# Probabilities times values in four 64x64 tiles of the array, the heads of a pair swapped for the second sequence

## The chip, the cores and the metric

The kernel runs on one core of one Trainium2 chip. The metric is the device time of one execution in microseconds (us). The engines are named as in the profile: PE is TensorE (PEld its weight loads), ACT is ScalarE, DVE is VectorE, POOL is GpSimd, SP is SyncE, which issues the transfers (SPq: the time it spends on issuing them).

## The reference, cut to what matters

Two attentions (streams a and c), a scan between them (stream b) and a mixture of experts (also stream c) run over 64 sequences of 64 positions with 256 features, all in float32. Each attention has 16 query heads of 64 and one shared key and value head, and one extra "null" key and value per sequence:

```python
sim = jnp.einsum('bhid,bjd->bhij', q, k) * SCALE + attn_bias   # masked
attn = jax.nn.softmax(sim, axis=-1)                            # (b, 16, 64, 65)
out = jnp.einsum('bhij,bjd->bhid', attn, v)                    # the product changed here
out = out.transpose(0, 2, 1, 3).reshape(b, n, INNER)
out = ln(out @ Wout, g_out)
```

## The kernel before

A tile of work is two sequences (`BT` = 2), 128 tokens on the 128 partitions; there are 32 tiles. The work is a software pipeline written out by hand: `ORDER` lists for every engine the steps of one iteration as `stream.step@lag`, and iteration i runs each step on tile i - lag, so five tiles are under way at once. Iterations 0 to 4 and the last four are unrolled, the middle is a loop. `Progress` counts the results of each engine and stream; a step waits until the count says that what it needs is there. `TURNS` gives the order in which steps use each of the eight PSUM banks, and after `>` the result of the engine that empties it; `Banks.free` (L251) turns that into a wait at the start of a PE step.

The steps around the change, in one iteration:

- PE: `... c.ex3 a.xt b.gt b.E0 a.O0 a.O1 b.E1 b.E2 b.E3 b.G a.kv a.W b.m0 b.m1 c.PT0 c.PT1 b.m2 c.O0 c.O1 b.m3 c.eb c.W b.yT`.
- ACT: `... a.PT0 a.PT1 b.BT a.xnT b.E0 a.O0 b.E0u a.O1 b.E1 c.expm b.E2 b.E3 c.prob c.PT0 c.PT1 c.O0 c.O1 a.rstd2`.

For an attention, `PT` (PE, L689) transposes the probabilities of eight pairs of heads, so that the partitions hold (head of the pair, key position); ACT copies them to `X.PT` (L946 to L951). DVE step `V` (L1175) puts the values of each sequence twice on the diagonal of a 128x128 block, in two instructions of 64 partitions. `PV(b)` (PE, L701, the product at L707) multiplies for sequence b that 128x128 block (stationary) with 128x512 of `X.PT` (moving: 8 pairs of heads by 64 positions) into bank `O{b}`; half of the products are with zeros. A float32 matmul is two instructions in the trace. `PV(b)` of ACT (L953 to L959) takes bank `O{b}`, all 128 partitions and 512 columns, to `X.OT`, adding the null value. `W` (PE, L711, L715) waits for ACT's `O1` and multiplies `X.OT` by the output weights in 8 matmuls.

Three turns of the banks matter. Bank 2 goes from `a.O0` to `b.E2`, once ACT's `O0` is done. Bank 1 holds `a.O1`. Bank 6 goes from `c.O0` to `c.eb` (L853), once ACT's `O0` is done. `b.E` (L784) are sums over log decays, `b.m` (L795) the products of the scan, `c.eb` the expert biases.

Of the neighbours: `BT` of ACT copies bank `b.gt` out in one copy of 128 partitions (L1034) and four of 32 (L1037), `b.E0`, `b.E1` ... are exponentials (L1050, `E0u` L1042), `c.prob` (L944) is the softmax exponential of stream c. It leads to DVE's sum and reciprocal (`den`, L1238 to L1243), to POOL's normalisation (`norm`, L1549) and to `c.PT0` (PE, L696). `qr` (ACT, L930 to L935) is the reciprocal norm of the queries of stream c, used by DVE's `c.S0` (L1213). `scores` (PE, L675, L683) already uses matmuls with 64 stationary columns, which write alternately to the partitions 0 to 63 (first sequence) and 64 to 127 (second). The biases are loaded by SP before the pipeline starts (L522, L579) and folded with the null bias by POOL (`fold_bias`, L1593).

Of the kernel before, what the change touches and what calls it, by code (L numbers as in the profile page):

```python
# [28 lines left out]
P = 128  # L29
# [29 lines left out]
def constants():  # L59
# [36 lines left out]
    for name, a in parts.items():  # L96
# [11 lines left out]
        b.bc@2 a.PT0@1 a.PT1@1 c.ex3@4 a.xt@0 b.gt@2 b.E0@2 a.O0@1 a.O1@1 b.E1@2 b.E2@2 b.E3@2  # L108
        b.G@2 a.kv@0 a.W@1 b.m0@2 b.m1@2 c.PT0@3 c.PT1@3 b.m2@2 c.O0@3 c.O1@3 b.m3@2 c.eb@4
# [31 lines left out]
        c.ks@3>dve.ks b.bc@2>dve.Ct a.xt@0>act.xnT a.kv@0>dve.V1 c.PT0@3>act.PT0 c.W@3>dve.cn""",  # L141
    1: """
        b.x@2>dve.xi c.xt@3>act.xnT c.kv@3>dve.V1 b.a@2>act.ae a.PT0@1>act.PT0 a.O1@1>act.O1
        b.yT@2>act.yT""",
    2: """
        b.z@2>dve.zi a.PT1@1>act.PT1 a.O0@1>act.O0 b.E2@2>act.E2 a.W@1>dve.cn""",
# [5 lines left out]
        c.PT1@3>act.PT1 c.O1@3>act.O1""",  # L152
# [4 lines left out]
        b.out@3>dve.x1 c.qs@3>dve.qs c.O0@3>act.O0 c.eb@4>dve.out""",  # L157
# [107 lines left out]
def build(nc, x, out, ins, consts_dram, consts_at):  # L265
    NT = x.shape[0] * x.shape[1] // P
    ctx = ExitStack()
    with ctx:
# [21 lines left out]
        for X, s in ((A, "a"), (C, "c")):  # L290
# [5 lines left out]
            X.null_bias = sb(f"{s}_null_bias", [P, H])  # L296
            X.bias = sb(f"{s}_bias", [P, H, S])
# [11 lines left out]
            X.V = sb(f"{s}_V", [P, BT, P])  # L309
# [136 lines left out]
        def load(eng, s, dst, src):  # L446
# [16 lines left out]
                                             for name in ("x_loaded", "xres_loaded", "out_stored"))  # L463
        A.bias_folded, C.bias_folded = sem("bias_folded_a"), sem("bias_folded_c")
# [35 lines left out]
        def _(sp):  # L500
# [3 lines left out]
            def load_weights():  # L504
# [65 lines left out]
            def position_bias():  # L570
# [7 lines left out]
                for b in range(BT):  # L578
                    sp.dma_start(C.bias[b * S:(b + 1) * S, :, :], skewed).then_inc(mlp_dma, 16)  # L579
# [32 lines left out]
        def _(pe):  # L612
# [9 lines left out]
            def attention(X):  # L622
# [78 lines left out]
                def PV(b):  # L701
                    def run(t):
                        pe.wait_ge(*banks.free(f"{s}.O{b}", t))
                        if b == 0:
                            pe.wait_ge(*dve.at("V1", t))
                            pe.wait_ge(*act.at("PT1", t))
                        pe.matmul(bank(f"O{b}")[:, :], X.V[:, b, :], X.PT[:, :, b * S:(b + 1) * S],  # L707
                                  start=True, stop=True).then_inc(p.done(f"O{b}"), 1)
                    return run

                def W(t):  # L711
                    pe.wait_ge(*banks.free(f"{s}.W", t))
                    pe.wait_ge(*act.at("O1", t))
                    for hp in range(HP):
# [5 lines left out]
                        "S1": scores(1), "PT0": PT(0), "PT1": PT(1), "O0": PV(0), "O1": PV(1), "W": W}  # L720
# [170 lines left out]
        def _(act):  # L891
# [6 lines left out]
            def attention(X):  # L898
# [23 lines left out]
                def q(half):  # L922
                    def run(t):
                        act.wait_ge(*p.at(f"q{half}", t))
                        act.wait_ge(*p.at("O1", t - 1))
                        act.copy(X.qT[:, 4 * half:4 * half + 4, :], banks[f"{s}.q{half}"][:, :])\  # L926
                           .then_inc(a.done(f"q{half}"), 1)
                    return run

                def qr_(t):  # L930
# [4 lines left out]
                    act.activation(qr[:, :], qr_l[:, :], ACT.Exp, scale=-0.5).then_inc(a.done("qr"), 1)  # L935
# [191 lines left out]
        def _(dve):  # L1127
# [7 lines left out]
            def attention(X):  # L1135
# [19 lines left out]
                def K(t):  # L1155
# [19 lines left out]
                def V(t):  # L1175
                    dve.wait_ge(*p.at("kv", t))
                    dve.wait_ge(*p.at("O1", t - 1))
# [24 lines left out]
                def scores(half):  # L1202
                    def run(t):
# [7 lines left out]
                        else:  # L1211
                            dve.wait_ge(*act.at("qr", t))
# [186 lines left out]
            def setup_weights(X, prep, scale):  # L1399
                for k in range(KD):  # L1400
# [20 lines left out]
            def setup_a():  # L1421
# [100 lines left out]
        def _(pool):  # L1522
# [70 lines left out]
            def fold_bias(X):  # L1593
                done = X.bias_folded
                pool.tensor_tensor(X.bias[:, :, :], X.bias[:, :, :],
                                   X.null_bias[:, :].unsqueeze(2).broadcast_to([P, H, S]), ALU.subtract)\
# [13 lines left out]
            def setup_c():  # L1610
                pool.wait_ge(ld_c, n_ld[ld_c.name])
                pool.wait_ge(mlp_dma, 16 + 16 * BT)
# [37 lines left out]
```

## Time and profile before

| | |
|---|---|
| three runs | 1917.19, 1923.50, 1925.61 us (median 1923.50) |
| profiled execution | 1921.49 us, its span 1919.7 us |
| mean granted TensorE clock | 0.966 of 2.4 GHz |
| PE busy | 1751.2 us (91% of the span), 11407 matmul instructions |
| PE weight loads | 1373.9 us (72%) |
| DVE / ACT / POOL busy | 1276.9 (67%) / 807.7 (42%) / 893.5 us (47%) |
| chain that ended last, by engine | PE 86%, DVE 4%, issue 3%, ACT 3%, POOL 2%, SPq 2% |
| L707 on that chain | part of PE's; its matmuls are busy for 61.9 us (a) and 62.2 us (c) |

A row of the timeline gives the start in us from the span's start, the duration, the engine, the line, the operation, out<-in by tile names, the stationary size (rows*columns) and the moving size for a matmul, xN for N instructions merged, and in brackets how long the engine had been idle and what ended that. The durations of pipelined instructions overlap: the next one starts before the one ahead of it ends.

### The profile page before, as it was taken

The page shows a single profiled execution, that of the slowest core. Times are in us where ns is not written, and L with a number is a line of the kernel's source. Part 1 is how long each engine was busy: PE and PEld are TensorE (multiplying, and loading weights), DVE is VectorE, ACT ScalarE, POOL GpSimd, SP SyncE. Part 2 cuts the span into 40 slices and gives each one's busy share as a digit, 9 for nine tenths or more (in the row PEclk, how much of TensorE's full clock was granted, in tenths as well). Part 3 has the DMA queues.
Part 4 walks back from the last instruction along what each step waited for, and adds up shares of the span by engine and source line. Part 5 has one row for each costly group of instructions (what it writes and reads, how often), then busy time and mean ns, then how long its engine had stood idle before and what let it go on. Part 6 is the DMA issues. An engine that isn't in the chain of part 4 may idle for free.

```text
span 1919.7 us, 37680 instructions
## 1 busy us (share of the span) xinstructions
PE 1751.2 (91%) x11407; PEld 1373.9 (72%) x11407; DVE 1276.9 (67%) x2684; ACT 807.7 (42%) x1943; POOL 893.5 (47%) x552
## 2 busy tenths in 40 slices
PE   2378999999999999999999999999999999999875
PEld 1256777777777777777777777778777777787644
DVE  3555766777777667777776667777766677776542
ACT  1134344444444444444444444444444444444321
POOL 1025445555544445555444555554445555544341
PEclk9678999999999999999999999999999999999986
DMA  7110000000000000000000000000000000000000
GB/s 210 53 25 6 2 10 10 9 9 5 4 9 9 9 9 9 9 6 3 9 9 9 9 9 9 6 2 9 9 9 9 9 9 7 1 9 7 6 4 5
DMA packets 40185, 26.52 MB, mean 14 GB/s; under 512 B 19786, under 2 KB 38226, under 8 KB 40148
## 3 DMA queue, kind: packets, MB, share of 16 engines
q1 hardware_dynamic: 40148, 26.05, 5.4%
q8 instruction: 20, 0.33, 0.1%
q14 instruction: 17, 0.14, 0.0%
HBM read 21.33 MB, written 4.71 MB: 14 GB/s over the span
## 4 chain that ended last, share of the span: by engine, by line
PE 86%; DVE 4%; issue 3%; ACT 3%; POOL 2%; SPq 2%; DMA 0%; POOLq 0%; DVEq 0%; ACTq 0%
PE bank L715 12%; PE bank L661 12%; PE bank L618 8%; PE bank L620 7%; PE bank L619 7%; PE bank L683 6%; PE bank L795 6%; PE bank L707 4%; PE bank L696 3%; PE bank L810 3%; PE bank L671 3%; PE bank L784 3%; PE bank L644 2%; PE bank L639 2%; SPq L448 2%
## 5 line engine op out<-in xcount | busy, mean ns | idle before, releaser
L1543 POOL TENSOR_TENSOR a_prob<-a_prob,a_mask 128x1024 f32<-128x1024 f32 x32 | 76.2, 2382 | 264.5 <-DVE a_prob L1209 264.5
L1582 POOL TENSOR_TENSOR y<-y,u 128x512 f32<-128x512 f32 x128 | 162.4, 1269 | 54.1 <-DVE u L1331 49.1
L1331 DVE TENSOR_TENSOR u<-bank,Ef 128x512 f32<-128x512 f32 x128 | 88.5, 691 | 135.8 <-PE bank L795 135.8
L1529 POOL TENSOR_TENSOR c_prob<-c_qT 128x1024 f32<-128x1024 f32 x32 | 82.3, 2573 | 160.4 <-ACT c_qT L926 160.4
L1562 POOL TENSOR_TENSOR resid<-xres,a_c 128x256 f32<-128x256 f32 x32 | 23.6, 738 | 267.8 <-DVE x L1339 215.5
L661 PE MATMUL bank<-a_xnT,a_wq 128*128 128x128 f32 x1024 | 129.2, 281 | 10.2 <-DVE gate_w_lo L1417 10.2
L795 PE MATMUL bank<-u,Gm 128*128 128x512 f32 x256 | 130.9, 613 | 7.8 <-DVE Gm L1323 4.5
L661 PEld LDWEIGHTS bank<-a_xnT,a_wq 128*128 128x128 f32 x1024 | 126.0, 198 | 13.3 <-issue 10.4
L1574 POOL TENSOR_TENSOR u<-xe,Ef 128x512 f32<-128x512 f32 x96 | 122.8, 1294 | 0.0
L715 PE MATMUL bank<-c_wo,c_prob 128*128 128x256 f32 x512 | 121.4, 391 | 0.0
L715 PE MATMUL bank<-a_wo,a_prob 128*128 128x256 f32 x512 | 119.1, 386 | 1.7 <-ACT Ef L1050 1.7
L661 PE MATMUL bank<-c_xnT,c_wq 128*128 128x128 f32 x1024 | 119.6, 275 | 0.0
L661 PEld LDWEIGHTS bank<-c_xnT,c_wq 128*128 128x128 f32 x1024 | 116.9, 192 | 0.0
L618 PE MATMUL bank<-w_e_hi,cT_hi 128*128 128x512 f32 x256 | 114.6, 448 | 0.7 <-ACT c_qT L926 0.7
L715 PEld LDWEIGHTS bank<-c_wo,c_prob 128*128 128x128 f32 x512 | 96.3, 193 | 23.7 <-issue 10.0
L1534 POOL TENSOR_TENSOR c_prob<-c_prob,c_bias 128x1024 f32<-128x1024 f32 x32 | 80.7, 2520 | 58.3 <-DVE c_prob L1213 58.3
L1549 POOL TENSOR_TENSOR a_prob<-a_prob,a_rden 128x1024 f32<-128x1024 f32 x32 | 61.4, 1918 | 98.0 <-DVE a_mask L1227 95.3
L949 ACT COPY c_qT<-bank 128x512 f32<-128x512 f32 x64 | 34.5, 589 | 172.4 <-PE bank L696 172.4
L715 PEld LDWEIGHTS bank<-a_wo,a_prob 128*128 128x128 f32 x512 | 94.6, 190 | 16.2 <-ACT Ef L1050 2.5
L620 PE MATMUL bank<-w_e_hi,cT_lo 128*128 128x512 f32 x256 | 102.2, 399 | 0.0
L619 PE MATMUL bank<-w_e_lo,cT_hi 128*128 128x512 f32 x256 | 101.8, 398 | 0.0
L1309 DVE TENSOR_TENSOR nl_lo<-yT,nl_hi 128x512 fp32r<-128x512 f32 x32 | 86.9, 2717 | 0.0
(289 smaller groups left out, 4658.1 us busy)
## 6 DMA issues: line engine op xcount, KB each, us to landing
a_xin<-in_x SPq DMA_DIRECT2D x32, 128.0 KB, 2.6
xres<-in_x SPq DMA_DIRECT2D x32, 128.0 KB, 2.5
out<-acc SPq DMA_DIRECT2D x32, 128.0 KB, 1.7
a_wq<-in_L_cond_Wq SPq DMA_DIRECT2D x1, 1024.0 KB, 5.0
a_wo<-in_L_cond_Wo SPq DMA_DIRECT2D x1, 1024.0 KB, 7.0
c_wq<-in_L_cond_Wq SPq DMA_DIRECT2D x1, 1024.0 KB
c_wo<-in_L_cond_Wout SPq DMA_DIRECT2D x1, 1024.0 KB
u<-in_L_ffn_expert_w SPq DMA_DIRECT2D x3, 256.0 KB, 3.9
```

Of the source, the lines that this page charges most:

```text
L618: pe.matmul(out, lhs[0][:, k, :], rhs[0], start=first, stop=False)
L619: pe.matmul(out, lhs[0][:, k, :], rhs[1], start=False, stop=False)
L620: return pe.matmul(out, lhs[1][:, k, :], rhs[0], start=False, stop=last)
L661: mm = pe.matmul(bank(f"q{half}")[:, m * P:(m + 1) * P], X.wq[:, k, hp * P:(hp + 1) * P], X.xnT[:, k, :], start=k == 0, stop=k == KD - 1)
L683: mm = pe.matmul(bank(f"S{half}")[b * S:(b + 1) * S, m * P:(m + 1) * P], X.qT[:, 4 * half + m, b * S:(b + 1) * S], X.K[:, b, :], start=Tru ...
L715: mm = pe.matmul(bank("W")[:, 0:D], X.OT[:, hp, :], X.wo[:, hp, :], start=hp == 0, stop=hp == HP - 1)
L795: pe.matmul(banks[f"b.m{l}"][:, :], Gm[:, l, :], u[l][:, :], start=True, stop=True).then_inc(p.done(f"m{l}"), 1)
L1309: dve.tensor_tensor(nl_parts[1][:, :], nl[:, :], nl_parts[0][:, :].bitcast(F32), ALU.subtract)\
L1331: dve.tensor_tensor(tm[l][:, :], banks[f"b.m{l}"][:, :], Ef[l][:, :], ALU.mult)\
L1529: pool.tensor_tensor(qsq[:, :, :], X.qT[:, :, :], X.qT[:, :, :], ALU.mult)\
L1574: pool.tensor_tensor(u[l][:, :], xi[:, :], (E0u if l == 0 else Ef[l])[:, :], ALU.mult)\
L1582: pool.tensor_tensor(y[:, :], y[:, :], tm[l][:, :], ALU.add).then_inc(g.done(f"y{l}"), 1)
```

## The change

The product becomes four matmuls of 64x64 stationary values by 64x512 of probabilities, one for each sequence and head of a pair; the values are stored once. For the second sequence the two heads of each pair change sides from the scores on, so that its products land on the other half of the partitions: key block, bias table, null bias and query norm are laid out for that. PE's two steps `O0` and `O1` become one step `O`, and a matmul of 32x64 by one column stands ahead of the four. ACT empties each bank in two instructions of 64 partitions.

```diff
 ORDER pe
-        ... b.E0@2 a.O0@1 a.O1@1 b.E1@2 ...   ... b.m2@2 c.O0@3 c.O1@3 b.m3@2 c.eb@4
+        ... b.E0@2 a.O@1 b.E1@2 ...           ... b.m2@2 c.O@3 b.m3@2 c.eb@4
 RESULTS act
-            "qr": "qr_l qr",
+            "qr": "qr_l qr0 qr1 qr2", "O0": "O00 O01", "O1": "O10 O11",
 TURNS
-        1: ... a.O1@1>act.O1       2: ... a.O0@1>act.O0      4: ... c.O1@3>act.O1      6: ... c.O0@3>act.O0
+        1: ... a.O1@1>act.O11      2: ... a.O0@1>act.O01     4: ... c.O1@3>act.O11     6: ... c.O0@3>act.O01
...
-            X.V = sb(f"{s}_V", [P, BT, P])
+            X.V = sb(f"{s}_V", [P, BT, DH])
...
-                    load(sp, ld_a, A.bias[part, :, :], ins["fside_16xSxS_0"].rearrange("h i j -> i h j"))
+                    table = ins["fside_16xSxS_0"].rearrange("h i j -> i h j")
+                    for n in range(1 + b):
+                        load(sp, ld_a, A.bias[part, n:H:1 + b, :], table[:, b - n:H:1 + b, :])
...
-                    sp.dma_start(C.bias[b * S:(b + 1) * S, :, :], skewed).then_inc(mlp_dma, 16)
+                    for n in range(1 + b):
+                        sp.dma_start(C.bias[b * S:(b + 1) * S, n:H:1 + b, :], skewed[:, b - n:H:1 + b, :])\
+                          .then_inc(mlp_dma, 16)
...
-                def PV(b):
-                    def run(t):
-                        pe.wait_ge(*banks.free(f"{s}.O{b}", t))
-                        if b == 0:
-                            pe.wait_ge(*dve.at("V1", t))
-                            pe.wait_ge(*act.at("PT1", t))
-                        pe.matmul(bank(f"O{b}")[:, :], X.V[:, b, :], X.PT[:, :, b * S:(b + 1) * S],
-                                  start=True, stop=True).then_inc(p.done(f"O{b}"), 1)
-                    return run
+                def PV(t):
+                    pe.wait_ge(*banks.free(f"{s}.O0", t))
+                    pe.wait_ge(*banks.free(f"{s}.O1", t))
+                    pe.wait_ge(*dve.at("V", t))
+                    pe.wait_ge(*act.at("PT1", t))
+                    pe.matmul(bank("O0")[0:DH, 0:1], X.V[0:32, 0, :], X.PT[0:32, 0, 0:1], start=True, stop=True)
+                    for b in range(BT):
+                        for half in range(2):
+                            rows, side = slice(half * S, (half + 1) * S), half if b == 0 else 1 - half
+                            mm = pe.matmul(bank(f"O{half}")[side * DH:(side + 1) * DH, :], X.V[rows, b, :],
+                                           X.PT[rows, :, b * S:(b + 1) * S], start=True, stop=True)
+                    mm.then_inc(p.done("O"), 1)
...
-                    pe.wait_ge(*act.at("O1", t))
+                    pe.wait_ge(*act.at("O11", t))
...
-                    act.activation(qr[:, :], qr_l[:, :], ACT.Exp, scale=-0.5).then_inc(a.done("qr"), 1)
+                    for n, (part, heads, of) in enumerate(((slice(0, S), slice(0, H), slice(0, H)),
+                                                           (slice(S, P), slice(0, H, 2), slice(1, H, 2)),
+                                                           (slice(S, P), slice(1, H, 2), slice(0, H, 2)))):
+                        act.activation(qr[part, heads], qr_l[part, of], ACT.Exp, scale=-0.5)\
+                           .then_inc(a.done(f"qr{n}"), 1)
...
-                def PV(b):
+                def PV(half):
                     def run(t):
-                        act.wait_ge(*p.at(f"O{b}", t))
-                        act.activation(X.OT[:, :, b * S:(b + 1) * S],
-                                       banks[f"{s}.O{b}"][:, :].rearrange("p (h i) -> p h i", h=HP),
-                                       ACT.Identity, bias=nv_col[:, :]).then_inc(a.done(f"O{b}"), 1)
+                        act.wait_ge(*p.at("O", t))
+                        for b in range(BT):
+                            side = half if b == 0 else 1 - half
+                            part = slice(side * DH, (side + 1) * DH)
+                            act.activation(X.OT[part, :, b * S:(b + 1) * S],
+                                           banks[f"{s}.O{half}"][part, :].rearrange("p (h i) -> p h i", h=HP),
+                                           ACT.Identity, bias=nv_col[part, :]).then_inc(a.done(f"O{half}{b}"), 1)
                     return run
...
-                        dst = X.K[part, :, half * S:(half + 1) * S]
+                        dst = X.K[part, :, :].rearrange("p b (q j) -> p (b q) j", j=S)[:, half:4 - half:3 - 2 * half, :]
...
-                    for half in range(2):
-                        part = slice(half * S, (half + 1) * S)
-                        dve.tensor_tensor(X.V[part, :, half * DH:(half + 1) * DH],
-                                          banks[f"{s}.kv"][part, P:2 * P].rearrange("p (b n) -> p b n", b=BT),
-                                          nv_row[part, :].unsqueeze(1).broadcast_to([S, BT, DH]),
-                                          ALU.subtract).then_inc(d.done(f"V{half}"), 1)
+                    dve.tensor_tensor(X.V[:, :, :], banks[f"{s}.kv"][:, P:2 * P].rearrange("p (b n) -> p b n", b=BT),
+                                      nv_row[:, :].unsqueeze(1).broadcast_to([P, BT, DH]),
+                                      ALU.subtract).then_inc(d.done("V"), 1)
...
             def setup_weights(X, prep, scale):
+                for part, heads, of in ((slice(0, S), slice(0, H), slice(0, H)),
+                                        (slice(S, P), slice(0, H, 2), slice(1, H, 2)),
+                                        (slice(S, P), slice(1, H, 2), slice(0, H, 2))):
+                    mm = dve.tensor_copy(X.null_swapped[part, heads], X.null_bias[part, of])
+                mm.then_inc(X.null_ready, 1)
...
-                dve.memset(A.V[:, :, :], 0.0)
-                dve.memset(C.V[:, :, :], 0.0)
...
             def fold_bias(X):
+                pool.wait_ge(X.null_ready, 1)
```

The rest of the diff renames the results that are waited for (`V1` to `V`, `O1` to `O`, `qr` to `qr2`) and reads `null_swapped` in `fold_bias`.

## Rows read from the trace of the kernel before

**Rows 1.** Windows, one iteration: busy us (instructions) of PE, PEld, DVE, ACT, POOL, clock.

```profile
740.00:794.80 54.80, 53.50 (x358) 42.17 (x357) 38.94 (x82) 24.97 (x60) 27.72 (x18) 1.00 0.02 7
```

**Rows 2.** Timeline of PE in that iteration, around `a.O0` and `a.O1`.

```profile
786.63 0.44 PE L632 MATMUL bank<-consts,a_xn 128*128 128x128 f32 x2 [1.05 <-DVE Ct L1317]
...
787.66 1.88 PE L707 MATMUL bank<-a_qT,a_V 128*128 128x512 f32 x4
...
790.18 0.50 PE L784 MATMUL bank<-nl_hi,sums 128*128 128x512 f32 x1 [0.17 <-ACT a_prob L956]
```

**Rows 3.** Timeline of ACT over the same stretch.

```profile
787.40 0.27 ACT L1034 COPY BTt<-bank 128x128 f32<-128x128 f32 x1 [2.53 <-PE bank L770]
787.56 1.09 ACT L1037 COPY CD<-bank 32x128 f32<-32x128 f32 x4
788.68 0.37 ACT L909 COPY a_xnT<-bank 128x256 f32<-128x256 f32 x1
788.95 0.60 ACT L1050 ACTIVATE Ef<-bank 128x512 f32<-128x512 f32 x1
789.44 0.69 ACT L956 ACTIVATE a_prob<-bank,nv_col 128x512 f32<-128x512 f32 x1
790.01 0.61 ACT L1042 ACTIVATE u<-bank 128x512 f32<-128x512 f32 x1
790.49 0.71 ACT L956 ACTIVATE a_prob<-bank,nv_col 128x512 f32<-128x512 f32 x1
...
791.64 1.12 ACT L1050 ACTIVATE Ef<-bank 128x512 f32<-128x512 f32 x2
792.59 1.11 ACT L944 ACTIVATE c_prob<-c_prob 128x1024 f32<-128x1024 f32 x1
```

**Rows 4.** Timeline of all engines around `c.O0`, `c.O1` and `c.W`.

```profile
800.58 1.88 PE L707 MATMUL bank<-c_qT,c_V 128*128 128x512 f32 x4
...
801.64 0.69 ACT L956 ACTIVATE c_prob<-bank,nv_col 128x512 f32<-128x512 f32 x1 [1.42 <-PE bank L707]
...
802.30 1.02 PE L795 MATMUL bank<-u,Gm 128*128 128x512 f32 x2
...
802.50 0.69 ACT L956 ACTIVATE c_prob<-bank,nv_col 128x512 f32<-128x512 f32 x1 [0.17 <-PE bank L707]
...
803.25 0.69 PE L853 MATMUL bank<-b_e,ohT 8*128 8x256 f32 x2
...
803.87 2.43 PE L715 MATMUL bank<-c_wo,c_prob 128*128 128x256 f32 x10
```

**Rows 5.** The chain that ended last, pieces of it: start, us.

```profile
745.96 1.72 PE bank L707 x4
...
762.17 1.78 PE bank L661 x16
763.96 1.02 PE bank L683 x16
...
778.23 1.68 PE bank L671 x16
```

**Rows 6.** Timeline of PE in a window of 60 ns where `a.S0` begins.

```profile
763.68 0.28 PE L661 MATMUL bank<-a_xnT,a_wq 128*128 128x128 f32 x1
763.89 0.33 PE L683 MATMUL bank<-a_K,a_qT 128*64 128x128 f32 x2
```

**Rows 7.** Timeline ahead of `c.PT0`: POOL's normalisation, DVE's `t0`, PE.

```profile
795.63 1.90 POOL L1549 TENSOR_TENSOR c_prob<-c_prob,c_rden 128x1024 f32<-128x1024 f32 x1 [0.77 <-DVE c_rden L1243]
...
797.94 0.69 DVE L1331 TENSOR_TENSOR u<-bank,Ef 128x512 f32<-128x512 f32 x1 [0.77 <-PE bank L795]
...
798.51 0.71 PE L696 MATMUL bank<-consts,c_prob 128*128 128x128 f32 x5
```

**Rows 8.** Timeline of ACT and DVE around `c.qr`.

```profile
780.70 0.22 ACT L935 ACTIVATE qr<-qr_l 128x16 f32<-128x16 f32 x1
...
781.91 0.68 DVE L1213 TENSOR_TENSOR c_prob<-bank,qr 128x512 f32<-128x512 f32 x1
```

**Rows 9.** Timeline of DVE: the values of stream c and what follows.

```profile
768.80 0.60 DVE L1180 TENSOR_TENSOR c_V<-bank,nv_row 64x128 f32<-64x128 f32 x2
770.02 0.29 DVE L1193 TENSOR_SCALAR kss<-bank 128x128 f32<-128x128 f32 x1 [0.62 <-PE bank L652]
```

**Rows 10.** Timeline of SP's issues before the pipeline.

```profile
9.24 1.37 SPq L448 DMA_DIRECT2D a_bias<-in_fside_16xSxS  x2
```

More of the change, by code:

```diff
@@ L107 @@
         c.xt@3 a.S1@1 c.kv@3 c.ex1@4 c.ks@3 c.q0@3 c.q1@3 b.a@2 c.ex2@4 c.qs@3 c.S0@3 c.S1@3
-        b.bc@2 a.PT0@1 a.PT1@1 c.ex3@4 a.xt@0 b.gt@2 b.E0@2 a.O0@1 a.O1@1 b.E1@2 b.E2@2 b.E3@2
-        b.G@2 a.kv@0 a.W@1 b.m0@2 b.m1@2 c.PT0@3 c.PT1@3 b.m2@2 c.O0@3 c.O1@3 b.m3@2 c.eb@4
+        b.bc@2 a.PT0@1 a.PT1@1 c.ex3@4 a.xt@0 b.gt@2 b.E0@2 a.O@1 b.E1@2 b.E2@2 b.E3@2
+        b.G@2 a.kv@0 a.W@1 b.m0@2 b.m1@2 c.PT0@3 c.PT1@3 b.m2@2 c.O@3 b.m3@2 c.eb@4
         c.W@3 b.yT@2""",
@@ L140 @@
     0: """
-        c.ks@3>dve.ks b.bc@2>dve.Ct a.xt@0>act.xnT a.kv@0>dve.V1 c.PT0@3>act.PT0 c.W@3>dve.cn""",
+        c.ks@3>dve.ks b.bc@2>dve.Ct a.xt@0>act.xnT a.kv@0>dve.V c.PT0@3>act.PT0 c.W@3>dve.cn""",
     1: """
-        b.x@2>dve.xi c.xt@3>act.xnT c.kv@3>dve.V1 b.a@2>act.ae a.PT0@1>act.PT0 a.O1@1>act.O1
+        b.x@2>dve.xi c.xt@3>act.xnT c.kv@3>dve.V b.a@2>act.ae a.PT0@1>act.PT0 a.O1@1>act.O11
         b.yT@2>act.yT""",
     2: """
-        b.z@2>dve.zi a.PT1@1>act.PT1 a.O0@1>act.O0 b.E2@2>act.E2 a.W@1>dve.cn""",
+        b.z@2>dve.zi a.PT1@1>act.PT1 a.O0@1>act.O01 b.E2@2>act.E2 a.W@1>dve.cn""",
     3: """
@@ L151 @@
         a.q0@1>act.q0 c.lg@4>dve.lb a.S0@1>dve.S0 c.ex1@4>dve.ac3 c.S1@3>dve.S1 b.E3@2>act.E3
-        c.PT1@3>act.PT1 c.O1@3>act.O1""",
+        c.PT1@3>act.PT1 c.O1@3>act.O11""",
     5: """
@@ L156 @@
     6: """
-        b.out@3>dve.x1 c.qs@3>dve.qs c.O0@3>act.O0 c.eb@4>dve.out""",
+        b.out@3>dve.x1 c.qs@3>dve.qs c.O0@3>act.O01 c.eb@4>dve.out""",
     7: """
@@ L296, in build @@
             X.null_bias = sb(f"{s}_null_bias", [P, H])
+            X.null_swapped = sb(f"{s}_null_swapped", [P, H])
             X.bias = sb(f"{s}_bias", [P, H, S])
@@ L463, in build @@
                                              for name in ("x_loaded", "xres_loaded", "out_stored"))
+        A.null_ready, C.null_ready = sem("null_ready_a"), sem("null_ready_c")
         A.bias_folded, C.bias_folded = sem("bias_folded_a"), sem("bias_folded_c")
@@ L719, in attention @@
                 return {"xt": xt, "kv": kv, "ks": ks, "q0": q(0), "q1": q(1), "qs": qs, "S0": scores(0),
-                        "S1": scores(1), "PT0": PT(0), "PT1": PT(1), "O0": PV(0), "O1": PV(1), "W": W}
+                        "S1": scores(1), "PT0": PT(0), "PT1": PT(1), "O": PV, "W": W}
             def scan():
@@ L924, in run @@
                         act.wait_ge(*p.at(f"q{half}", t))
-                        act.wait_ge(*p.at("O1", t - 1))
+                        act.wait_ge(*p.at("O", t - 1))
                         act.copy(X.qT[:, 4 * half:4 * half + 4, :], banks[f"{s}.q{half}"][:, :])\
@@ L1176, in V @@
                     dve.wait_ge(*p.at("kv", t))
-                    dve.wait_ge(*p.at("O1", t - 1))
-                    for half in range(2):
-                        part = slice(half * S, (half + 1) * S)
-                        dve.tensor_tensor(X.V[part, :, half * DH:(half + 1) * DH],
-                                          banks[f"{s}.kv"][part, P:2 * P].rearrange("p (b n) -> p b n", b=BT),
-                                          nv_row[part, :].unsqueeze(1).broadcast_to([S, BT, DH]),
-                                          ALU.subtract).then_inc(d.done(f"V{half}"), 1)
+                    dve.wait_ge(*p.at("O", t - 1))
+                    dve.tensor_tensor(X.V[:, :, :], banks[f"{s}.kv"][:, P:2 * P].rearrange("p (b n) -> p b n", b=BT),
+                                      nv_row[:, :].unsqueeze(1).broadcast_to([P, BT, DH]),
+                                      ALU.subtract).then_inc(d.done("V"), 1)
                 def kc(t):
@@ L1211, in run @@
                         else:
-                            dve.wait_ge(*act.at("qr", t))
+                            dve.wait_ge(*act.at("qr2", t))
                             dve.tensor_tensor(X.prob[:, heads, :], src,
@@ L1594, in fold_bias @@
                 done = X.bias_folded
+                pool.wait_ge(X.null_ready, 1)
                 pool.tensor_tensor(X.bias[:, :, :], X.bias[:, :, :],
-                                   X.null_bias[:, :].unsqueeze(2).broadcast_to([P, H, S]), ALU.subtract)\
+                                   X.null_swapped[:, :].unsqueeze(2).broadcast_to([P, H, S]), ALU.subtract)\
                     .then_inc(done, 1)
@@ L1611, in setup_c @@
                 pool.wait_ge(ld_c, n_ld[ld_c.name])
-                pool.wait_ge(mlp_dma, 16 + 16 * BT)
+                pool.wait_ge(mlp_dma, 16 + 16 * 3)
                 fold_bias(C)
```

4 rows, old and new, of the table RESULTS are left out of this document.

## The prediction, written before the changed kernel was run

> **What bounds the kernel now.** I read the page first: PE has most of the chain that ended last. Then the windows: in an iteration of 54.80 us PE is busy for 53.50 us, at a granted clock of 1.00, the upper of its two levels, 2.4 GHz [rows 1]. So a us more or less on PE's path counts in full, and an engine that is busy for less than half of the time, as ACT with 24.97 us, costs nothing on average. An average does not tell who ends a wait, though, so I read the timeline at the two places where the product stands.
>
> At the first, `a.O0` and `a.O1`, PE has had a wait of 1.05 us for DVE, then runs on. ACT starts its row of work at 787.40 and from there has no gap: one copy, four small ones, `a.xnT`, `b.E0`, and then `a.O0` [rows 3]. PE starts `b.E2` at 790.18, after a wait of 0.17 us that ACT's L956 ended [rows 2]: bank 2 is free only when ACT has emptied `a.O0`, at 789.44 + 0.69 = 790.13. So here ACT, not PE, already sets the time of `b.E2`, and the product's own PE time is covered by that.
>
> At the second place PE runs `c.O0`, `c.O1`, `b.m3`, `c.eb`, `c.W` without a gap from 800.58 to 803.87, which is 3.29 us, while ACT empties the two banks from 801.64 and from 802.50 and ends at 803.19 [rows 4]. `c.W` needs that end; it has 0.68 us to spare. Here PE is the limit, but ACT is close behind.
>
> **What the change removes: PE time of the product.** Now it is 1.72 us for four instructions, 0.43 each [rows 5]. That tiles of the array run at the same time is shown by the scores: 16 instructions with 64 stationary columns take 1.02 us, 16 with 128 columns and the same 128 moving columns 1.78 us [rows 5], and the first two of them start within 60 ns of each other, before either can have streamed [rows 6]. Nothing in the trace has 64 rows as well. Bounds: all four tiles together is 2 x 0.43 = 0.86 us, none together 8 x 0.43 = 3.44 us. I take 0.86, as the two directions split one array and the four products touch four different pairs of row half and bank half. Going into tiles and out of them costs 1.02 - 8 x 0.11 = 0.14 us (0.11 being 1.78 / 16), of which I put 0.07 ahead of the product and 0.07 behind.
>
> **What it adds on PE: the one-column matmul.** Two more instructions of another tile size. The nearest row is the 128x2 product, 1.68 / 16 = 0.105 us an instruction [rows 5]. I take 0.2 us; bounds 0.1 and, with a second change of tile size, 0.35. So the step is 0.2 + 0.86 + 0.14 = 1.2 us against 1.72: 0.5 us less of PE's own time, 64 times.
>
> **What it adds on ACT: the second half of the work.** Two instructions of 128 partitions become four of 64, with the same 512 columns. Partitions do not shorten a copy: the four copies of 32 partitions stand 1.09 / 4 = 0.27 us each, the one of 128 partitions, with the same 128 columns, 0.27 us [rows 3]. So each new instruction is a full one: it holds ACT for 790.01 - 789.44 = 0.57 us before the next starts and ends after 0.69. Bounds: 0.28 if half the partitions were half the time, 0.60. I take 0.57.
>
> **First place, worked out.** ACT's row up to `a.O0` does not depend on the product (its matmuls are over before 789.44). Bank 2 is now free after two instructions: 789.44 + 0.57 + 0.69 = 790.70, so `b.E2` starts at 790.75 instead of 790.18: **+0.57 us**. The 0.5 us saved on PE makes the wait longer, nothing else. Behind it: ACT's `b.E2` and `b.E3` start 2 x 0.57 = 1.14 later, at 792.78, and the bank of `a.W` is free at about 793.4, while PE comes to it at about 793.9. `c.prob` starts at 793.7 instead of 792.59 [rows 3], and with it sum, reciprocal and POOL's normalisation, which now ends at 797.53 [rows 7], later by 1.14, at 798.67. `c.PT0` starts at 798.51 now [rows 7] and at 799.08 then: a margin of 0.4, no further wait, but this is what is late next. In tile 0 this place is a chain of latencies and in tile 1 ACT is less full; I count 0.3 each for them, and tile 31 adds nothing. 29 x 0.57 + 0.6 = 17.1 us.
>
> **Second place, worked out.** From the start s of the product: 0.2 + 0.07 + 0.43 to the start of the last pair of instructions; ACT starts 0.63 later (now 801.64, with the second instruction of `c.O0` at 800.58 + 0.43 [rows 4]), at s + 1.33. Its fourth instruction starts 3 x 0.57 later and ends after 0.69: s + 3.73. `c.W` follows 0.05 later, as `b.E2` did [rows 2, 3]: s + 3.78 against s + 3.29 now: **+0.49 us**. `b.m3` and `c.eb` fill only part of that; `c.eb` waits too, for two instructions of ACT instead of one. Had ACT been free, it would have been 0.5 less. This holds for 31 tiles: 15.2 us. In the last tile the clock is at its lower level and PE's time for the old product is twice as long, which covers the new ACT time: nothing.
>
> **What lies beside other work.** `c.qr` becomes three instructions: two more of at most 0.22 us, ending at 781.4 at the latest, and DVE reads it at 781.91, held by its own work until then [rows 8]. DVE's `V` is one instruction instead of two, a gain of 0.3 us, which ends in a wait of DVE for PE both times, 0.62 us behind `c.V` and 0.77 before `b.t0` [rows 7, 9]: nothing. `K` writes other columns at the same size. In the setup SP issues one more DMA ahead of everything that follows on its queue, the load of the second tile's input too, on which the first pipeline stage hangs: a bias DMA takes 1.37 / 2 = 0.68 us to issue [rows 10] (between 0, if halves cost half, and 0.68; I take 0.68). The second new DMA, for stream c's bias, comes at a point where POOL is still at earlier steps. Three small DVE copies ahead of the weights of stream c are on the path of the setup: 0.1 us each, at most 0.22 as ACT's 128x16 [rows 8]; for stream a they fall into the time of the SP queue. Two memsets fall away where DVE waits for the loads anyway. Setup: +1.0 us.
>
> **Sum.** 17.1 + 15.2 + 1.0 = 33.3 us on the profiled execution's 1921.5: 1954.8 us. The median of the three runs lies 2 us above that execution, so 1955 to 1957; I say 1955. With all bounds of this case (ACT 0.50 to 0.60, the small matmul 0.1 to 0.35) it is 1946 to 1962. A measurement of this kernel can tell about 0.5%, 10 us, from no change.
>
> **Rivals.** *Only two tiles at a time* (0.12). The trace only ever shows two. The product is then 4 x 0.43 = 1.72 plus 0.34. At the second place all ends 0.86 later (+1.35). At the first, ACT gets its bank at 787.66 + 0.27 + 1.29 + 0.63 = 789.85 instead of 789.44 (+0.98). Sum 31 x 2.33 + 1 = 73: 1994 us.
>
> *The two instructions of one matmul follow each other and nothing overtakes* (0.06). Then the second of each overlaps only with the first of the next: five steps of 0.43, 2.14 us, 0.43 more at both places than the last case: 2021 us. Against it stands that two instructions of the scores start together [rows 6], which two halves on the same tile could not. The Trainium skill states this rule ("TensorE: Matmul & The Clock Gate", section "The mechanism"): matmuls start and end in program order, with no reordering. Taken with adjacent halves it would give this time; the row speaks for halves that are interleaved across tiles.
>
> *ACT's halves are cheap* (0.08, the other side). If a 64-partition instruction held ACT for x us, the first place would move by x and the second by 0.49 + 4 (x - 0.57), but not below PE's own saving of 0.5. The sum is zero at x = 0.36; below 0.15 it is a gain that can be told, and at 0.1 it is 31 x (0.1 - 0.5) + 1 = -11 us: 1910 us. For it: no row has a 64-partition ACTIVATE. Against it: the copies of 32 partitions.
>
> *No change* (0.12): x near 0.36, or waits elsewhere (the 1.05 us for DVE in rows 2) that shrink by what is added here; against that, DVE's work ahead of that wait starts from a PE result [rows 9], so it shifts along: 1923 us.
>
> **Chances.** Main case 0.62. The range of 1934 to 1996 leaves out the last two cases' fast parts and the second rival. Slower: 0.62 + 0.12 + 0.06 = 0.80; same 0.12; faster 0.08.
>
> **What would show it.** ACT's L956 at 256 instructions of 64 partitions and about 0.69 us each; L707 in steps of 0.43 us with four instructions started together; before `b.E2` a PE wait near 1.2 us for L956 instead of 0.17; before `c.eb` and `c.W` new waits for L956; an iteration of about 55.85 us; PE busy down, ACT busy up by about 75 us. Wrong it would be if the iteration shortened, if L956 were much below 0.6 us, or if the growth were in `c.PT0`'s wait for POOL.

## The result, and the profile after

The changed kernel takes 2017.16 us (median of 4 runs, 2007.72 to 2024.73) against 1924.55 us before (4 runs): 1.0487 times as long, 95% interval 1.0423 to 1.0550. The forecast was 1955 us, with a range up to 1996. The direction was right, the size was not: about three times the forecast loss. The profiled execution took 2007.72 us (span 2005.9 us), 86.2 us more than the profiled one of before.

Windows of two iterations of the changed kernel, an early and a later one, in the columns of [rows 1]:

```profile
376.81:433.27 56.46, 53.22 (x369) 41.30 (x369) 38.28 (x80) 28.00 (x67) 27.20 (x18) 1.00 0.03 7
772.05:830.08 58.03, 54.79 (x368) 42.39 (x368) 38.24 (x80) 27.95 (x67) 27.16 (x18) 0.97 0.02 7
```

There are two losses to read. Already the early iteration takes 56.46 us instead of 54.79 (from one start of `c.W` to the next; the window of [rows 1] is rounded to 54.80), 1.67 us more, with PE less busy and ACT 3 us busier. The later one takes 58.03 us and has a mean clock of 0.97. Iterations are of the first kind until 772 us and of the second from there to 1817 us.

Timeline of PE at both places, in the early iteration (the counterpart of [rows 2] and [rows 4]):

```profile
357.87 0.44 PE L638 MATMUL bank<-consts,a_xn 128*128 128x128 f32 x2 [0.88 <-DVE Ct L1330]
...
359.00 0.27 PE L712 MATMUL bank<-a_qT,a_V 32*64 32x1 f32 x2
359.20 1.09 PE L716 MATMUL bank<-a_qT,a_V 64*64 64x512 f32 x8
...
362.11 0.50 PE L793 MATMUL bank<-nl_hi,sums 128*128 128x512 f32 x1 [1.15 <-ACT a_prob L972]
...
365.29 3.72 PE L724 MATMUL bank<-a_wo,a_prob 128*128 128x256 f32 x16
...
372.73 0.27 PE L712 MATMUL bank<-c_qT,c_V 32*64 32x1 f32 x2
372.93 1.09 PE L716 MATMUL bank<-c_qT,c_V 64*64 64x512 f32 x8
373.95 1.12 PE L804 MATMUL bank<-u,Gm 128*128 128x512 f32 x2
375.53 0.69 PE L862 MATMUL bank<-b_e,ohT 8*128 8x256 f32 x2 [0.46 <-ACT c_prob L972]
```

PE did what was hoped: from the start of the small matmul to the start of `b.m3` it is 373.95 - 372.73 = 1.22 us, instead of 1.72 (a further 0.2 us is lost just outside this stretch, see the first experiment). All of the gain, and more, is in the waits: 1.15 us before `b.E2` (it was 0.17), 0.46 before `c.eb` and 0.59 before `c.W`, where there had been none. All three wait for L972, ACT's emptying of the banks. Timeline of ACT over the same stretch, the counterpart of [rows 3]:

```profile
360.18 0.60 ACT L1066 ACTIVATE Ef<-bank 128x512 f32<-128x512 f32 x1
360.67 1.38 ACT L972 ACTIVATE a_prob<-bank,nv_col 64x512 f32<-64x512 f32 x2
362.08 0.60 ACT L1058 ACTIVATE u<-bank 128x512 f32<-128x512 f32 x1
362.71 1.39 ACT L972 ACTIVATE a_prob<-bank,nv_col 64x512 f32<-64x512 f32 x2
...
374.08 2.67 ACT L972 ACTIVATE c_prob<-bank,nv_col 64x512 f32<-64x512 f32 x4 [1.81 <-PE bank L716]
```

The second loss is in the later iterations. Timeline of PE around `c.W`, and the clock over it:

```profile
828.80 0.69 PE L862 MATMUL bank<-b_e,ohT 8*128 8x256 f32 x2 [0.46 <-ACT c_prob L972]
830.09 5.41 PE L724 MATMUL bank<-c_wo,c_prob 128*128 128x256 f32 x16 [0.59 <-ACT c_prob L972]
```

```profile
830.00:832.00 2.00, 1.92 (x6) 1.52 (x7) 1.34 (x3) 0.42 (x3) 1.77 (x2) 0.64 0.18 66
832.00:834.00 2.00, 2.00 (x6) 1.62 (x5) 0.22 (x1) 1.01 (x4) 0.00 (x0) 0.51 0.37 51
```

The same 16 matmuls that take 3.72 us in `a.W` take 5.41 us in `c.W`. From 830.6 to 834.0 us the granted clock is at its lower level, 1.2 GHz, right behind the two waits. That costs 58.03 - 56.46 = 1.57 us in each of eighteen iterations, up to 1817 us.

**Where the 86.2 us are.** By the starts of `c.W`: 6.7 up to the first (202.05 before, 208.74 after); 16.3 over the next ten iterations; 58.4 over eighteen of the second kind, of which 18 x 1.67 = 30.1 is the first loss and 18 x 1.57 = 28.3 the clock; 5.8 over the last three; 1.0 less behind them.

### The profile page after: what moved, and what is told of

It is laid out like the page before. It is cut to its first block, busy times and chain, and to the rows that moved or that the text cites. A ratio compares the mean times of both kernels' runs of the same rounds, so it can differ in the third digit from the quotient of the medians.

```text
span 2005.9 us, 38750 instructions
## 1 busy us (share of the span) xinstructions
PE 1772.7 (88%) x11791; PEld 1369.4 (68%) x11791; DVE 1254.3 (63%) x2624; ACT 903.5 (45%) x2135; POOL 878.1 (44%) x552
## 4 chain that ended last, share of the span: by engine, by line
PE 69%; issue 10%; ACT 8%; POOL 5%; DVE 4%; SPq 2%; POOLq 0%; ACTq 0%; DMA 0%; DVEq 0%
PE bank L667 11%; PE bank L724 9%; PE bank L624 8%; PE bank L626 7%; PE bank L625 7%; PE bank L689 6%; POOL u L1590 4%; ACT c_prob L972 3%; PE bank L819 3%; PE bank L677 3%; PE bank L804 2%; PE bank L716 2%; PE bank L793 2%; ACT a_prob L972 2%; PE bank L702 2%
## 5 line engine op out<-in xcount | busy, mean ns | idle before, releaser
L724 PE MATMUL bank<-c_wo,c_prob 128*128 128x256 f32 x512 | 153.7, 467 | 20.0 <-ACT c_prob L972 20.0
L724 PEld LDWEIGHTS bank<-c_wo,c_prob 128*128 128x128 f32 x512 | 118.9, 237 | 55.6 <-ACT c_prob L972 33.5
L972 ACT ACTIVATE c_prob<-bank,nv_col 64x512 f32<-64x512 f32 x128 | 83.9, 679 | 59.9 <-PE bank L716 58.3
```

Source lines behind the costliest of these rows:

```text
L724: mm = pe.matmul(bank("W")[:, 0:D], X.OT[:, hp, :], X.wo[:, hp, :], start=hp == 0, stop=hp == HP - 1)
L972: act.activation(X.OT[part, :, b * S:(b + 1) * S], banks[f"{s}.O{half}"][part, :].rearrange("p (h i) -> p h i", h=HP), ACT.Identity, bias= ...
```

## The experiments

Ratios are to runs of the kernel before on the same chip. Iteration lengths are read as above. First, which part of the change costs the time.

**ACT in two full instructions**

```diff
-                        for b in range(BT):
-                            ...
+                        act.activation(X.OT[:, :, half * S:(half + 1) * S],
+                                       banks[f"{s}.O{half}"][:, :].rearrange("p (h i) -> p h i", h=HP),
+                                       ACT.Identity, bias=nv_col[:, :]).then_inc(a.done(f"O{half}1"), 1)
```

> The changed kernel, but ACT empties each of the two banks in one instruction of 128 partitions, as before (128 instead of 256 in all). It leaves out the placing of the second sequence's heads: they land in other columns, so what W multiplies is not the attention's output, at the same cost. Theory (the loss is ACT's second pair of instructions, and the low clock that follows from PE's waits for them): b.E2 waits as before, the second place gains PE's 0.5 us, the clock stays at its upper level in the steady part, an iteration takes about 54.3 us and the whole about 1907 us (1900 to 1916). Rival (the tiled product itself, its small matmul or the changes of tile size cost the time): over 1950 us.

Measured: 1915.08 us, ratio 0.9948 (0.9931 to 0.9966), iteration 54.33 us, clock 1.00. All of the product in tiles is still there, and the loss is gone; what remains is a gain of 0.46 us an iteration. The rival is out. The total is 8 us above the 1907 that I expected, at the upper end of the range. Timeline of ACT at the second place, and the window of one iteration:

```profile
800.55 1.27 ACT L969 ACTIVATE c_prob<-bank,nv_col 128x512 f32<-128x512 f32 x2 [1.81 <-PE bank L716]
```

```profile
747.77:802.10 54.33, 52.91 (x370) 41.27 (x369) 38.34 (x80) 25.17 (x62) 27.57 (x17) 1.00 0.02 8
```

ACT empties both banks in 1.27 us where the change needs 2.67.

Here PE has no wait at the second place, so its own gain can be read. Timeline of PE, this kernel first, the kernel before second:

```profile
798.14 1.12 PE L804 MATMUL bank<-u,Gm 128*128 128x512 f32 x2
799.20 0.27 PE L712 MATMUL bank<-c_qT,c_V 32*64 32x1 f32 x2
799.40 1.09 PE L716 MATMUL bank<-c_qT,c_V 64*64 64x512 f32 x8
800.41 1.12 PE L804 MATMUL bank<-u,Gm 128*128 128x512 f32 x2
801.47 0.69 PE L862 MATMUL bank<-b_e,ohT 8*128 8x256 f32 x2
```

```profile
799.62 1.12 PE L795 MATMUL bank<-u,Gm 128*128 128x512 f32 x2
800.58 1.88 PE L707 MATMUL bank<-c_qT,c_V 128*128 128x512 f32 x4
802.30 1.02 PE L795 MATMUL bank<-u,Gm 128*128 128x512 f32 x2
803.25 0.69 PE L853 MATMUL bank<-b_e,ohT 8*128 8x256 f32 x2
```

The product with its small matmul takes 1.21 us instead of 1.72, but `b.m2` ahead of it takes 1.06 instead of 0.96 until the next step starts, and `b.m3` behind it 1.06 instead of 0.95. From `b.m2` to `c.eb` PE takes 3.33 us instead of 3.63: its gain is 0.30 us, not 0.50. The rest of the 0.46 is there before the first place, where `a.xt` starts 37.39 us after `c.W` instead of 37.55; no run shows why.

**The kernel before, with ACT's halves alone**

```diff
-                        act.activation(X.OT[:, :, b * S:(b + 1) * S],
-                                       ...
+                        for half in range(2):
+                            part = slice(half * DH, (half + 1) * DH)
+                            act.activation(X.OT[part, :, b * S:(b + 1) * S],
+                                           banks[f"{s}.O{b}"][part, :].rearrange("p (h i) -> p h i", h=HP),
+                                           ACT.Identity, bias=nv_col[part, :]).then_inc(a.done(f"O{b}{half}"), 1)
```

> The kernel before, with its 128x128 product, but ACT empties each bank in two instructions of 64 partitions: the ACT part of the change alone. Theory: b.E2 0.7 us later, c.W 0.6 us later, iteration about 56.1 us; PE is busy for 1 us more than in the changed kernel, so I expect no low stretch of the clock: about 1963 us. If the low clock comes here too, about 1990. Rival (the tiled product costs the time): about 1925 us.

Measured: 1973.52 us, ratio 1.0248 (1.0225 to 1.0272), iteration 56.50 us. The ACT part alone makes the first loss, without any tile of 64 rows. The iteration is 0.4 us longer than expected, and the total 10 us. The low clock does not come: PE is as late as in the changed kernel, but at the second place it waits only once, for 0.55 us, where the changed kernel waits 0.46 and 0.59. Timeline of PE:

```profile
826.65 0.69 PE L853 MATMUL bank<-b_e,ohT 8*128 8x256 f32 x2
827.90 0.48 PE L715 MATMUL bank<-c_wo,c_prob 128*128 128x256 f32 x1 [0.55 <-ACT c_prob L958]
```

The windows from 800 to 1600 us, the changed kernel first, then this one (clock behind the bracket of POOL):

```profile
800.00:1600.00 800.00, 754.65 (x5039) 582.80 (x5038) 525.91 (x1087) 385.40 (x909) 376.93 (x237) 0.97 0.03 7
```

```profile
800.00:1600.00 800.00, 758.60 (x5062) 596.59 (x5060) 554.97 (x1149) 396.58 (x902) 387.47 (x241) 1.00 0.03 7
```

**The same, with halves of columns instead of partitions**

```diff
-                            part = slice(half * DH, (half + 1) * DH)
+                            hps = slice(4 * half, 4 * half + 4)
+                            act.activation(X.OT[:, hps, b * S:(b + 1) * S],
+                                           banks[f"{s}.O{b}"][:, 256 * half:256 * half + 256]
...
```

> The kernel before, with its 128x128 product, but ACT empties each bank in two instructions of 128 partitions and 256 columns: as many instructions as in the changed kernel, on half the columns each instead of half the partitions. Theory (an ACT instruction costs by its columns, not its partitions, and follows its predecessor with an overlap of 0.1 us only where both begin at the same partition): each takes about 0.40 us, the second starts 0.3 us after the first, a pair takes as long as one full instruction did, so there is no loss: 1920 to 1932 us. Rival (the loss is a price per instruction or per semaphore increment): about 1973 us, as with the halves of 64 partitions.

Measured: 1928.31 us, ratio 1.0017 (1.0000 to 1.0034). As many instructions and as many results to count, and no loss that the times can tell (in the traces the iteration is 54.93 us, 54.79 before). The instructions take 0.47 to 0.50 us rather than 0.40. All four of stream c take 1.70 us, although the second bank comes later:

```profile
751.86 1.70 ACT L958 ACTIVATE c_prob<-bank,nv_col 128x256 f32<-128x256 f32 x4 [1.42 <-PE bank L707]
```

So the price is not per instruction: it is that half the partitions take as long as all. The overlap part of this theory has no experiment of its own, only rows: two instructions of 64 partitions that start at different partitions take 1.38 us (the changed kernel), two of the same size that both start at partition 0 take 1.26 us (ACT in the fourth kernel shared with DVE, below). The four at the second place of the changed kernel start at 374.08, 374.79, 375.38 and 376.08 us: 0.71 and 0.70 apart where the start partition changes, 0.59 where it stays.

**Filling PE's waits, to hold the clock**

```diff
-        b.m3@2 c.eb@4
+        b.m3@2 c.fill@3 c.eb@4
...
+                def fill(t):
+                    pe.wait_ge(*banks.free(f"{s}.W", t))
+                    pe.matmul(bank("W")[:, D:2 * D], ident, X.wo[:, 0, :], start=True, stop=True)\
+                      .then_inc(p.done("fill"), 1)
...
                 def W(t):
                     pe.wait_ge(*banks.free(f"{s}.W", t))
+                    if s == "c":
+                        pe.matmul(bank("W")[:, D:2 * D], ident, X.wo[:, 0, :], start=True, stop=True)
```

> The changed kernel with two more 128x256 matmuls of PE per iteration, of constants into unused columns of W's bank, one ahead of c.eb and one ahead of c.W, where PE waits for ACT (0.46 and 0.59 us; each matmul 0.43 us). Theory (from about 780 us on, PE's waits bring the clock down for one stretch of 3.4 us in each iteration, and c.W runs in it): with the waits filled the clock stays up, the iteration stays at 56.5 us to the end, and the whole is about 1980 us although PE does more. Rival (c.W takes 5.4 us for another reason, or the filling is added work): 2008 to 2035 us.

Measured: 1974.99 us, ratio 1.0259 (1.0234 to 1.0283), iteration 56.34 us to the end. More work on PE makes the changed kernel 42 us faster, by medians. The window from 800 to 1600 us against that of the changed kernel above:

```profile
800.00:1600.00 800.00, 768.25 (x5301) 595.59 (x5300) 545.77 (x1124) 395.61 (x936) 387.32 (x242) 1.00 0.03 7
```

The low clock is thus a consequence of PE's waits at the second place, and nothing else had made `c.W` slow. This splits the loss: about half is ACT, half the clock.

**Only stream c changed.** Stream a's product, values, scores and emptying are as before; stream c's are as in the changed kernel.

```diff
-                def V(t): ...
+                    if s == "c":
+                        ...
-            ... c.O0@3 c.O1@3 ...      (PE)
+            ... c.O@3 ...              (a.O0@1 a.O1@1 kept)
```

> Stream a as before the change, stream c as in the changed kernel (ACT alone, four instructions). Theory (each place pays for itself): c.W 0.8 us later after the product, nothing at stream a's place: iteration 55.6 us, total about 1948 us, with the clock at its upper level in the steady part since only one of the two places has PE waiting. Rival (the low clock comes from stream c's waits, which stand right ahead of the stretch in which it fell): it comes here too, iteration over 56.5 us, total over 1975 us.

Measured: 1960.99 us, ratio 1.0196 (1.0165 to 1.0226). Most iterations take 55.67 us, as expected. Both theories miss the rest: the low clock comes, but in single iterations only, as in the first of these two neighbours:

```profile
482.62:539.96 57.34, 55.13 (x363) 42.84 (x363) 38.52 (x81) 26.38 (x65) 27.57 (x18) 0.97 0.03 7
539.96:595.64 55.68, 53.47 (x363) 41.71 (x363) 38.53 (x81) 26.38 (x65) 27.57 (x18) 1.00 0.04 7
```

So stream c's waits alone can bring it down, and stream a's are not needed for that. Over all kernels of this document, the low clock comes in the steady part only in the three where PE waits 0.46 and 0.59 us at the second place (the changed one, this one, and the next); where it waits there once, for 0.46 or 0.55 us, or not at all, it never does.

**What would undo the loss.** At the first place, `a.kv` of PE (1.06 us) can go into the wait.

```diff
-        ... a.O@1 b.E1@2 b.E2@2 b.E3@2 b.G@2 a.kv@0 a.W@1 ...
+        ... a.O@1 b.E1@2 a.kv@0 b.E2@2 b.E3@2 b.G@2 a.W@1 ...
```

> The changed kernel with a.kv (1.06 us of PE) moved ahead of b.E2, into the wait for ACT's emptying of bank 2 (1.15 us). Theory: that wait nearly goes, but c.PT0 then comes 1.0 us earlier while POOL's normalisation does not, so 0.5 to 0.6 us of it comes back as a wait there: 0.45 us less per iteration, 1994 us with the low clock, about 1965 without. Rival (PE's order does not matter because the chain ACT, DVE, POOL sets the pace of this place): within 5 us of 2008.

Measured: 2009.10 us, ratio 1.0431 (1.0407 to 1.0456), iteration 56.45 and later 58.03 us. The rival holds (the profiled run of the changed kernel took 2007.72 us), though the wait that came back is one that I had not named. Timeline of PE in this kernel:

```profile
364.56 0.60 PE L645 MATMUL bank<-a_xnT,a_wkk 128*128 128x128 f32 x4
365.89 0.50 PE L793 MATMUL bank<-nl_hi,sums 128*128 128x512 f32 x1
...
369.07 3.72 PE L724 MATMUL bank<-a_wo,a_prob 128*128 128x256 f32 x16 [1.12 <-ACT Ef L1066]
```

`b.E2` has no wait left that these rows show, but it starts no earlier (41.77 us after `c.W` in both kernels), and `a.W` waits 1.12 us: it uses the same bank 2, which ACT empties from `b.E2` (L1066) only behind all four instructions of `a.O`. ACT's whole row sets the pace here, not the one bank.

Then ACT's row was shortened by giving part of it to DVE. The kernels, each built on the last: DVE empties `c.O1`; DVE also empties `a.O1`; the same with `a.kv` moved; the same with stream c shared by partitions.

```diff
 ORDER dve
-        ... b.t2@2 b.t3@2 ...
+        ... b.t2@2 c.O1@3 b.t3@2 ...
 (second kernel)
-        ... c.mx@3 c.sub@3 b.Gm@2 ...
+        ... c.mx@3 c.sub@3 a.O1@1 b.Gm@2 ...
...
+                            dve.tensor_scalar(X.OT[part, :, b * S:(b + 1) * S],
+                                              banks[f"{s}.O1"][part, :].rearrange("p (h i) -> p h i", h=HP),
+                                              nv_col[part, :], None, ALU.add).then_inc(d.done(f"O1{b}"), 1)
```

> The changed kernel, but DVE empties bank c.O1 (two instructions of 64 partitions, between b.t2 and b.t3, where it is idle for 1.9 us); ACT keeps c.O0 and both banks of stream a. Theory: c.eb still waits for ACT's two instructions on bank 6, so c.W starts about 3.4 us after the product instead of 4.1 (before: 3.3); stream a's place keeps its 0.9 us; the shorter waits keep the clock up: iteration about 55.8 us, total about 1953 us. Rival (ACT's work for stream a alone makes all of the loss): no less than 2000 us.

> As the kernel before it, and DVE also empties bank a.O1 (after c.sub, ahead of b.Gm). ACT then has two instructions in each place, as before the change. Theory: b.E2 still waits for the second half of a.O0, 0.7 us more than before the change, but ACT's row behind it is as long as it was, so a.W has no wait of its own: iteration about 55.6 us, total about 1947 us.

> As the kernel before it, with a.kv of PE ahead of b.E2. When a.kv was moved alone, a.W took over the wait, for ACT's emptying of b.E2's bank behind four instructions of a.O. With ACT's row shortened by two, the theory expects that wait gone and PE's 0.5 us of gain to show: iteration about 54.6 us, total about 1915 us. Rival (PE's order still does not matter): as the kernel before it.

> As the kernel before it, but in stream c ACT takes partitions 0 to 63 of both banks and DVE 64 to 127 of both, at the same time, so that c.eb waits for one instruction of each and c.W for two. Theory: PE runs from the product to c.W without a wait, 2.8 us instead of 3.3 before the change; with stream a's place 0.3 us shorter, an iteration takes about 54.0 us and the total is about 1898 us, faster than both kernels (ratio to before about 0.987). Rival (ACT and DVE on one bank slow each other, or POOL's normalisation becomes the wait): 1910 to 1925 us.

| | median, us | ratio (interval) | iteration, us (expected) |
|---|---|---|---|
| DVE empties `c.O1` | 1957.40 | 1.0187 (1.0163 to 1.0211) | 55.7 (55.8) |
| and `a.O1` | 1958.95 | 1.0191 (1.0166 to 1.0215) | 55.7 (55.6) |
| and `a.kv` first | 1926.52 | 1.0031 (1.0015 to 1.0046) | 54.6 (54.6) |
| and stream c by partitions | 1919.31 | 0.9983 (0.9968 to 0.9997) | 54.43 (54.0) |

The iteration comes out as expected in three of four. The same move of `a.kv` that was worth nothing with ACT's row at full length is worth 1.05 us an iteration once that row is short. The totals are 4 to 21 us above what was expected. Where DVE empties `a.O1`, part of that is in the last iterations: the third from the end takes 59.6 us in the second and third kernel and 57.7 in the fourth, 54.6 before. In the last kernel ACT and DVE work on one bank at the same time, and `c.eb` comes without a wait of PE:

```profile
745.19 1.26 ACT L979 ACTIVATE c_prob<-bank,nv_col 64x512 f32<-64x512 f32 x2 [1.81 <-PE bank L716]
745.19 1.43 DVE L1272 TENSOR_SCALAR c_prob<-bank,nv_col 64x512 f32<-64x512 f32 x2 [0.47 <-PE bank L716]
...
746.11 0.69 PE L868 MATMUL bank<-b_e,ohT 8*128 8x256 f32 x2
```

**Stream a as before, stream c shared.** Built from the kernel before and the last one's stream c.

```diff
-                    dve: one V, K, O path for both streams
+                    if s == "a": as before the change; else: product in tiles,
+                    ACT partitions 0 to 63 and DVE 64 to 127 of both banks
```

> Stream a as before the change (128x128 product, ACT one instruction for each bank); stream c in four tiles, its two banks emptied by ACT (partitions 0 to 63) and DVE (64 to 127) at the same time. Theory: PE goes from the product to c.W in 2.9 us instead of 3.3, stream a's place stays as before, and the last iterations lose nothing to a longer DVE row: iteration 54.4 us, total about 1910 us, ratio to before about 0.994. Rival (part of stream a's change was a gain that is lost here): 1919 us or more.

Measured: 1919.31 us, ratio 0.9982 (0.9967 to 0.9998), iteration 54.66 us. That is the rival's time, though its reason is not what the rows show. From the product to `c.W` PE takes 0.4 us less than before, but only 0.13 of it is left over the iteration. Timeline of PE behind `c.W`, this kernel first, the kernel before second:

```profile
748.76 3.72 PE L736 MATMUL bank<-c_wo,c_prob 128*128 128x256 f32 x16
...
755.03 0.44 PE L846 MATMUL bank<-consts,c_c 128*128 128x128 f32 x2
```

```profile
749.09 3.72 PE L715 MATMUL bank<-c_wo,c_prob 128*128 128x256 f32 x16
...
755.08 0.40 PE L825 MATMUL bank<-consts,c_c 128*128 128x128 f32 x2
```

`c.ct` comes 6.27 us after `c.W` instead of 5.99: 0.28 us are given back there, where PE's weight load now waits for DVE's `c_c`. Of that, 0.19 is left by `a.xt`, and 0.10 goes into the longer `b.m2` ahead of the tiles. The fourth kernel pays the same two items: `a.xt` 0.31 us later after `c.W` than before, and 0.10 at `b.m2`; that is the 0.4 us by which its 54.43 exceeds the 54.0 expected. Neither this kernel nor the last can be told from the kernel before by the 0.5% that I set.

## Why the prediction was right and wrong

**Four tiles at once, 0.86 us: right, but PE's gain was 0.3 and not 0.5 us.** Four matmuls start together, their second instructions together 0.48 us later; with the small matmul 1.22 us, where the sum had 1.20 with 0.14 for the changes of tile size in it. These changes cost another 0.10 us ahead of the small matmul and 0.10 in `b.m3`, so the step is 1.42 us. At the first place ACT covers that. Timeline of PE in a window of 60 ns, the counterpart of [rows 6]:

```profile
372.93 0.66 PE L716 MATMUL bank<-c_qT,c_V 64*64 64x512 f32 x4
```

The result lies near the time of the second rival (2021 us), but its mechanism is out: with the halves of a float32 matmul one behind the other, these four could not have started together. The Trainium skill's rule ("TensorE: Matmul & The Clock Gate", "The mechanism"), that matmuls start in program order, holds only if the second halves are counted as behind all four first ones; by the adjacent order the product would have taken 2.14 us, and it took 0.86 and the entry. The first rival (two tiles at a time) is out by the same row.

**ACT's halves cost full instructions: right, and it is the first loss.** The rival of cheap halves is out: 0.68 us each.

**The step of 0.57 us: the term that was mis-sized.** The prediction had: "it holds ACT for 790.01 - 789.44 = 0.57 us before the next starts". That was the step between two instructions over all partitions. The pair of halves takes 1.38 us, so the step is 1.38 - 0.68 = 0.70, and behind the pair ACT does not overlap either: the next starts 1.41 us after the pair's start (362.08 - 360.67). The rows had it: the four copies of 32 partitions stand 0.27 us apart and take 0.26 each, without an overlap [rows 3], and I had used that very row to show that partitions don't shorten a copy. At the second place, the four take 2.67 us instead of the 3 x 0.57 + 0.69 = 2.40. The band of 1946 to 1962 did not cover this either; its lower end also leaves out the bound of the small matmul (with it, 1943).

**The first place, +0.57: measured +0.80.** Once the iterations have settled, `b.E2` starts 0.67 later, counted from `c.W` (41.77 against 41.10 us), and `a.W` another 0.13 later (44.95 against 44.15): that "the bank of `a.W` is free at about 793.4, while PE comes to it at about 793.9" had taken ACT's row 0.3 us too short. The move of `a.kv` showed that this margin was gone.

**The second place, +0.49: measured +0.79** from the product to `c.W` (4.08 us against 3.29), **and 0.10 ahead of it**, in `b.m2`. With stream c alone changed the iteration grows by 0.88, the same two items. Sum of both places: 1.69, which is the whole 1.67 us per iteration within the reading, where I had 1.06.

**The clock: left out.** I had read a clock of 1.00 [rows 1] and carried it over to a kernel in which PE waits longer at three points. The sum had no term for it, and no rival either. It cost 28 us here, half of what was missing. A row did bear on it: in the epilogue, where PE waits, the clock before was at its lower level, and I used that for the last tile only. The four runs differ by the same cause, as far as their mean clocks tell: 0.950 and 2008 to 2010 us twice, 0.942 and 2024 to 2025 us twice. Ten more iterations with the drop would be 10 x 1.57 = 15.7 us, about that difference, but that it begins earlier in the slower two is argued, not seen.

**The start, +1.0: measured 6.7 to the first `c.W`.** It contains ACT's cost in the first tiles, which I had put elsewhere. What the setup cost is not shown. In the first experiment, with ACT as before, the first `c.W` came 3.4 us later than before (205.44); but with the halves of columns, which leave the setup as it was, it came 3.6 us later (205.64). PE's first matmul with `a_wq` starts 0.6 us later in the changed kernel (30.86 against 30.23) and 0.4 later in that one (30.67). One trace of each kernel does not resolve the 1.0 us.

**What was covered was covered.** `c.qr`, `V` and `K` made no wait that the trace shows. `c.PT0` did not wait for POOL in the steady part; it had the margin that I gave it.

Open: why the drop of the clock comes back in each iteration once it has begun, but only now and then with stream c alone changed; why it begins only after ten iterations with the same waits; and what the setup cost.

## What to carry to other kernels

When a change splits a result over more, narrower tiles, price its emptying first: on ACT an instruction of 64 partitions took as long as one of 128 with the same 512 columns (0.68 and 0.69 us), and in these rows the next one overlapped it only where both began at the same partition. Here 0.3 us of gain on PE bought 1.4 us of ACT at the second place, and ACT was the one waited for though it was busy for 45% of the time. The Trainium skill says that tiling speeds up TensorE but not the emptying of PSUM, and to use both ScalarE and VectorE for that ("TensorEngine Tiling (Array Packing)", "PSUM Bottleneck"); the kernels shared with DVE bear it out, from 1.049 down to 1.019, and to 0.998 with `a.kv` moved and the partitions of stream c shared. None of them is clearly faster than the kernel before.

A forecast that adds waits to PE needs a term for the clock: 1.05 us of wait, in two pieces, right ahead of 3.7 us of matmuls made those take 5.4 in eighteen iterations, though not in the ten before them. Two idle matmuls in these waits took 2% off.

## What the runs showed that I had not expected

Adding PE work made the kernel faster, 2017 to 1975 us. ACT and DVE can empty the same bank at the same time on different partitions at 0.68 and 0.75 us an instruction, the same as where each has a bank to itself (within 0.01 us). And the two instructions of a float32 matmul do not follow each other when other tiles are free: four first halves start before any second one, all within 0.02 us.
